# A mixture of experts with two choices per token: gathers that wait for the transpose five places ahead of them

## The reference, cut to what matters

```python
def _L2_ffn_ref(x, router_w, w1, w2):        # 2048 tokens, D = 128, H = 512, E = 8
    xf = x.reshape(-1, d)
    probs = jax.nn.softmax(xf @ router_w.T, axis=-1)
    topv, topi = jax.lax.top_k(probs, 2)
    topv = topv / (topv.sum(axis=-1, keepdims=True) + 1e-09)
    cw = (jax.nn.one_hot(topi, e, dtype=xf.dtype) * topv[..., None]).sum(axis=1)
    h = jax.nn.gelu(jnp.einsum('td,edh->teh', xf, w1), approximate=False)
    y = jnp.einsum('teh,ehd->ted', h, w2)
    out = jnp.einsum('te,ted->td', cw, y)
    return out.reshape(b, s, d)
...
x = x + 0.5 * _L2_ffn_ref(_layernorm(x, axis=-1), ...)      # step 6
x = x + _L2_attn_ref(_layernorm(x, axis=-1), ...)           # step 7
x = x + 0.5 * _L2_ffn_ref(_layernorm(x, axis=-1), ...)      # step 8
```

## Time and profile before

| | us |
|---|---|
| median of three runs | 1728.9 |
| the profiled execution, its own time | 1739.16 |
| its span, first to last instruction | 1737.3 |
| PE busy | 1432.1 (82%) |
| DVE busy | 1196.4 (69%) |
| ACT busy | 1112.7 (64%) |
| POOL busy | 460.4 (27%) |
| mean granted clock of TensorE, as a share of full speed | 0.892 |

### The profile page before, as it was taken

One profiled execution on the slowest core, in us unless ns is written; L12 is line 12 of the kernel. 1 busy time (PEld: TensorE's weight loads), 2 busy tenths in 40 slices (PEclk: granted clock), 3 DMA queues, 4 the chain that ended last, 5 costly groups with the idle time before them and its releaser, 6 DMA issues. The chain is left out here.

```text
span 1737.3 us, 29542 instructions
## 1 busy us (share of the span) xinstructions
PE 1432.1 (82%) x9181; PEld 840.7 (48%) x9239; DVE 1196.4 (69%) x2827; ACT 1112.7 (64%) x2522; POOL 460.4 (27%) x610
## 2 busy tenths in 40 slices
PE   4797668999999695674799999897488787999989
PEld 4345555777777584673222222223388452222245
DVE  6576645877887637225899999995422676999566
ACT  3554647988888563343499888886244434888833
POOL 1231434333433343352130211111345000122100
PEclk8798788999999696896699999999599896999979
DMA  2002223130300343012330303003111304323000
GB/s 81 5 1 98 77 77 112 35 74 1 74 1 1 97 126 94 25 41 75 84 86 1 85 2 105 1 1 122 31 32 38 100 7 114 78 75 77 1 1 25
DMA packets 75077, 93.81 MB, mean 54 GB/s; under 512 B 11200, under 2 KB 61504, under 8 KB 74544
## 3 DMA queue, kind: packets, MB, share of 16 engines
q1 hardware_dynamic: 67088, 77.27, 15.7%
q0 software_dynamic: 6144, 12.60, 2.5%
q10 hardware_dynamic: 1696, 2.10, 0.5%
HBM read 57.22 MB, written 34.70 MB: 53 GB/s over the span
## 5 line engine op out<-in xcount | busy, mean ns | idle before, releaser
L2387 DVE TENSOR_REDUCE MAXI<-psum 128x1 f32<-128x512 f32 x768 | 473.0, 683 | 37.9 <-PE psum L2108 33.8
L2276 ACT ACTIVATE BIG<-psum 128x512 f32<-128x512 f32 x768 | 410.9, 608 | 62.4 <-PE psum L2129 55.8
L2108 PE MATMUL psum<-KM,QS 64*128 64x512 bf16 x768 | 256.7, 404 | 41.0 <-DVE MAXI L2387 25.3
L2129 PE MATMUL psum<-QM,KM 64*128 64x512 bf16 x768 | 235.2, 389 | 2.2 <-DVE REST L2377 1.9
L2139 PE MATMUL psum<-BIG,VST 128*32 128x512 f32 x1536 | 205.4, 607 | 4.9 <-ACT OT L2290 4.2
L2974 DVE TENSOR_TENSOR LOWS<-EX,HIGHS 128x1024 fp32r<-128x1024 f32 x128 | 158.3, 1240 | 61.4 <-POOL HIGHS L3030 31.9
L1215 PE MATMUL psum<-m_XT,m_W 128*128 128x128 f32 x992 | 148.7, 298 | 31.4 <-DVE m_XT L1482 26.0
L2916 ACT ACTIVATE EX<-psum 128x512 f32<-128x512 f32 x256 | 153.7, 608 | 17.9 <-PE psum L2831 17.9
L2108 PEld LDWEIGHTS psum<-KM,QS 64*128 64x128 bf16 x768 | 57.0, 94 | 223.6 <-DVE MAXI L2387 194.9
L3030 POOL CAST HIGHS<-EX 128x512 fp32r<-128x512 f32 x128 | 109.1, 853 | 179.0 <-ACT EX L2916 114.6
L1215 PEld LDWEIGHTS psum<-m_XT,m_W 128*128 128x128 f32 x992 | 135.2, 211 | 39.6 <-DVE m_XT L1482 30.0
(11 more groups left out here) (363 smaller groups left out, 2539.3 us busy)
## 6 DMA issues: line engine op xcount, KB each, us to landing
BIG<-in_w_dram SPq DMA_DIRECT2D x24, 512.0 KB
parts<-PART SPq DMA_DIRECT2D x24, 384.0 KB, 2.6
parts<-PART SPq DMA_DIRECT2D x24, 256.0 KB, 2.3
rows<-N SPq DMA_DIRECT2D x16, 256.0 KB, 2.8
N<-y SPq DMA_DIRECT2D x16, 256.0 KB, 4.3
QS<-parts SPq DMA_DIRECT2D x32, 128.0 KB, 3.8
QS<-parts SPq DMA_DIRECT2D x14, 256.0 KB, 5.6
parts<-PART SPq DMA_DIRECT2D x24, 128.0 KB, 1.8
```

The source lines that it names most:

```text
L2108: last = pe.matmul(peaks_at(PK * n + i)[:, k, :], QS[r, buf, g, qt * P:(qt + 1) * P], KM[r, buf, g, m, :], start=True, stop=True)
L2129: pe.matmul(bank_of(("score", n, i)), KM[r, buf, g, m, kt * P:(kt + 1) * P], QM[r, n % 2, MAPS[at] // slots, :], start=True, stop=True).th ...
L2276: act.activation(EX[n % 2][:, kt, MAPS[j], :], bank_of(("score", n, i)), ACT.Exp, scale=SM_SCALE).then_inc(S["exp"].sem, 1)
L2387: dve.tensor_reduce(MAXI[:, n % 2, qt, columns], peaks_at(PK * n + i), AX, ALU.max, negate=True).then_inc(S["reduced"].sem, 1)
```

## The change

The wait of a gather gets a constant of its own, PACE. It is 3 with one choice, where AHEAD was 3 as well, so nothing changes there. With two choices it is 5, where AHEAD is 18: gather r now waits until tile r - 5 has been turned, from `gather(5)` on. The ring keeps its 18 places, and the order of transfers on POOL is the same.

```diff
         AHEAD, DEEP, COPIED = 3 if one else 18, 5, 4
-        STEPS = 3 if one else 4
+        STEPS, PACE = 3 if one else 4, 3 if one else 5
...
                 def gather(r):
-                    if r >= AHEAD:
-                        pool.wait_ge(S["turned"].sem, S["turned"].at(r - AHEAD + 1))
+                    if r >= PACE:
+                        pool.wait_ge(S["turned"].sem, S["turned"].at(r - PACE + 1))
```

## The result

The changed kernel takes 1702.4 us, the median of five runs (1700.2 to 1708.1), beside 1733.0 us (1728.7 to 1736.8) of the kernel before in five runs, three of which are those that the prediction knew: a ratio of 0.983, with a 95% interval of 0.980 to 0.986. That is 30.7 us, or 1.8%, less. The forecast was 1703.5.

What follows compares the result with a forecast made beforehand. POOL's 18 gathers without a gap were taken to delay PE's signals and stop the other engines. 11.2 + 1.45 = 12.7 us a stage, 25.4 us for two, off the median 1728.9 gives 1703.5 us; range 1699 to 1707.

Steps and rivals of the forecast that it cites:

- What bounds the kernel: Two-choice loops: during POOL's 18 gathers without a gap PE's signals come late; the stop ends with that run.
- the second case: At gather 9 the signal of turn(4) is late for POOL too; POOL stops, which lets the signals through.
- The 11.2 us: POOL's first run ends nine gathers earlier, so everything behind it moves forward by 11.2 us a stage.
- The clock: PE's fall to 1.2 GHz after the stop costs 2.9 us; half, 1.45 us a stage, was taken as gained.
- The stretch of pairs: Gathers 18 to 31, alternating with scatters: the later turn asked for changes 0, plus or minus 2 us a stage.
- The median: Total time: 25.4 us less than the median of 1728.9 us gives 1703.5 us.
- A late gather: Gathers issued five steps (9.5 us) ahead of their turn, data taking about 3 us: none late, no cost.
- The weighed rule on DVE's copies: GpSimd cannot write descriptors during DVE's fp32 SBUF copies; a gather would take some 4.7 us; the trace disagreed.
- Rival 1: Two-choice loops: no stop remains at all, 17.5 us less a stage, 1693.9 us; chance 0.20.
- Rival 3: The stop has another cause, a fixed place in the program, and stays; 1729 us, no change; chance 0.13.
- Rival 4: The stop stays and gathers slow seven loop steps by 1.3 us each, 9.1 a stage; 1747 us; chance 0.06.
- Rival 2: Part of the stop, at most 10.3 us of the 25.4, exists only while recording; 1713.8 us; chance 0.16.

Runs made afterwards that it cites:

- e2: The changed kernel with PACE 9 instead of 5 in the two-choice stages; 1719.5 us, ratio 0.991 to the kernel before.
- e3: The changed kernel with PACE 13 instead of 5 in the two-choice stages; 1731.6 us, ratio 1.000 to the kernel before.
- e5: The kernel before with a small POOL fill and a wait for it behind each of gathers 5 to 16, two-choice stages; 1704.1 us, ratio 0.981.
- e11: The changed kernel as it is, run again on chip 8; 1707.7 us, ratio 0.983 to the kernel before.
- e1: The changed kernel with PACE 3 instead of 5 in the two-choice stages; 1701.7 us, ratio 0.981 to the kernel before.
- e9: The kernel before with constants for the two-choice register loads on PE, ACT and DVE, on chip 6; 1674.5 us, ratio 1.001.
- e10: The kernel before with a constant for the two-choice register load on PE alone, on chip 6; 1682.2 us in one run.
- e7: The changed kernel, but behind the first 18 gathers three gathers then one scatter, the scatters left last; 1712.0 us, ratio 0.985 to the kernel before.
- e8: The changed kernel, but all 32 gathers, paced, ahead of all scatters; 1712.7 us, ratio 0.986 to the kernel before.
- e4: The kernel before with two POOL fills and a wait for them behind gather 8 alone, in two-choice stages; 1729.2 us, ratio 0.997.
- e12: The kernel before with constants for the two-choice register loads on PE, ACT and DVE, on chip 8; 1722.3 us, ratio 0.991.

## Why the prediction was right, point by point

- **What bounds the kernel: right.** Beside POOL's run of transfers the others stop, and the stop ends shortly after the run. e2 and e3 move the end of the run, and the stop follows; e5 breaks the run up by fills that know nothing of PE, and the stop is gone.
- **The new wait at `gather(9)`: the second case, as taken.** The signal of `turn(4)` is late for POOL too (2.05 us, "remote"). POOL then rests, and the signal reaches it and DVE. From first gather to `xt(4)`, 23.33 us became 12.82 in step 6 and 24.06 became 12.81 in step 8. The 11.2 us thus came as 10.5 and 11.3: in step 6 the signal needs 1.8 us after the last gather's end, and not 1.1 as before.
- **The clock: the term was too small.** Half of 2.9 us was taken, since PE would still rest. It rested 1.03, 0.54 and, before `up(5)`, 0.95 us and stayed at its upper level. The rest of 2.4 us before `up(4)`, on which the half was founded, did not come, since DVE received `turn(4)` and `turn(5)` together. From `xt(4)` to the first scatter 3.7 and 2.3 us were gained in steps 6 and 8, where 1.45 were forecast. 14.2 and 13.6 us a stage were measured, 27.8 in all where 25.4 were forecast. That 11.2 + 2.9 = 14.1 comes so near is in part luck, for in step 6 the two terms were off by 0.7 and 0.8 us in opposite directions, and in step 8 the second fell 0.6 us short.
- **The stretch of pairs: no gain shown.** 0 with plus or minus 2 us a stage was taken; -0.7 and -2.3 came, the latter just outside. These 3 us and the 2.4 above (27.8 - 25.4) are the 5.3 us by which the measured 30.7 exceed the forecast 25.4, but for rounding. But the second trace of the change (e11) has 75.14 and 75.46 us there, no less than the kernel before, so they need not come from the change.
- **The median: nearly right by luck, for the gain was 5 us too small.** The forecast started from 1728.9, the median of three runs; with two more it is 1733.0. 1728.9 - 30.7 would be 1698.2, outside the forecast's own range of 1699 to 1707.
- **A late gather: none,** as said; even three steps ahead are enough (e1).
- **The weighed rule on DVE's copies: it stays as the trace had it.** Beside DVE's work a gather takes 0.94 us after the change too. The 4.7 us were a poor test of the rule: they stretched the gather by a ratio, while a gather that waited for the end of one of DVE's copies (0.23 us) could lose no more than that. The trace shows a small effect the other way round. Such a copy takes 0.38 us, and ends 0.05 us after the gather, where it begins shortly before the end of one; this one stands beside the gather of 698.30 to 699.24:

```profile
698.91 0.38 DVE L1482 COPY m_XT<-m_XR 128x128 f32 x1 [0.32 <-issue]
```

- **Rival 1, no stop at all, fell:** a remote wait of 2.91 us stays. Its price of 17.5 us was sound as a price of `y(7)`: with pace 3, which has next to no remote wait before it, `y(7)` comes 43.06 - 26.08 = 17.0 us earlier. Its slip is that the first scatter can't follow at once where a paced `gather(17)` stands ahead of it, and so gains 14.2 us in e1.
- **Rival 3, another cause, fell** with the result. **Rival 4, gathers beside the loop, fell:** from 698 to 706 POOL issues one gather per step, and PE keeps its full rate.
- **Rival 2, a stop that the recording makes, is not settled,** and its bound was badly founded. Twenty-three runs of the kernel before on one chip lie between 1727.4 and 1742.0 us, so the 10.3 us between the profiled execution and the median was spread from run to run and bounded nothing. Each run's span and clock are themselves taken from a record; no run here was without one. The traces speak rather for this rival than against it, for they lose records where the stop is. The landing of an indirect transfer is told by 16 raises of a semaphore, 3072 for the 192 transfers. The trace of the kernel before holds 1183 of them, that of the change 1248, and the ten others from chips 11, 4 and 8 hold 1137 to 1311. The two of chip 6 hold 3049 and 3050. The view of transfers shows it too, since it gives the time to landing only where no raise is missing; here are the gathers of the kernel before and, behind them, those of e9:

```profile
m_XG<-rows,m_ROWS POOLq DMA_INDIRECT x96
```

```profile
m_XG<-rows,m_ROWS POOLq DMA_INDIRECT x96, 2.6
```

  So chip 6, without a stop, is no case of the same recording. Either the recording holds the signals back on the other chips, or what delays them there also loses records; only runs without a record could tell, and they would also tell whether the 1.8% is there without one.

What stays open: by which path POOL's transfers hold up TensorE's signals on three chips of four, whether by their issuing or by their data, whether they would do so unrecorded, and what the change does on a chip like number 6. It was not run there, and since its traces show no such stop, no gain should be assumed for it. The stretch of pairs has late signals as well: in the changed kernel ACT waits 10.5 us for remote signals between 708 and 752 us. It needs 43.98 us for 14 pairs (3.14 each), where e10 on chip 6 has a pair every 2.57 us. e1, with 70.99 us from first scatter to last, is the best seen of it on the other chips with this order and these loads.

## What to carry to other kernels

Where GpSimd issues many indirect transfers, look at what the *other* engines do during the longest row of them that has no gap: waits of over 2 us that end by a "remote" signal, together with that row's end, are the sign. Break the row up, by a wait for progress or by small filler work of about 0.5 us with a wait for it (both gave the same), and look at the whole queue: e7 and e8 only moved the row to its end. Measure what you want to move: the first scatter hid 2.8 us of what `y(7)` had gained in e1. Run both kernels on several chips before crediting a change, and without the recording if you can, since the stop cured here does not exist on each chip and was seen only in recorded runs.

## What the runs showed of the hardware

- Beside gathers or scatters that POOL issues every 1.25 to 1.28 us, DVE and ACT waited 8 to 16 us for signals of TensorE on chips 4, 8 and 11, in recorded runs. Beside a gather every 1.77 us (e5) they did not.
- POOL's being busy does not do it: beside a fill of 1.82 us the signal came through (e4).
- One chip of four ran the kernel before in 1676.4 us, the others in 1732.2 to 1738.5 us. These 3.2 to 3.6% are larger than any effect tried here. Its traces alone hold nearly all the raises of semaphores (3049 and 3050 of 3072 for indirect transfers, against 1137 to 1311).
- Without register loads the time falls by 0.9% on a chip with the stop (e12) and not at all on the one without it (e9).
- A copy of DVE from m_XR to m_XT takes 0.23 us, and 0.38 us where it meets the end of a gather.
